# Attention loop: two steps' value products in one TensorE block, maxima over two PSUM banks, output multiply on GpSimd, three q/k buffers

## The chip, the cores and the metric

One NeuronCore of one Trainium2 chip runs the whole kernel. The metric is the device time of an execution in microseconds (us). TensorE is written PE, VectorE DVE, ScalarE ACT, GpSimd POOL and SyncE SP, as the profile does.

## The reference

The program is one graph-attention layer, a transformer layer with modulated layer norms, and an MLP, on x of 2 x 2048 x 512. The change touches only the self-attention of the second layer, 16 heads of 32 columns over 2048 positions:

```python
q, k, v = jnp.moveaxis(qkv, 2, 0)
scale = HD ** (-0.5)
attn = jnp.einsum('blhd,bmhd->bhlm', q, k) * scale
attn = jax.nn.softmax(attn, axis=-1)
out = jnp.einsum('bhlm,bmhd->blhd', attn, v).reshape(B, L, D)
```

## The kernel before

The kernel is a chain of phases (set-up, graph attention, q/k/v projection, attention, output projection, MLP); each ends in a barrier. Only the attention phase is changed.

**Groups, halves, steps.** A group is one pair of heads of one batch entry: `NG` = 16 groups. A group has `ST` = 32 steps in two halves of `MT` = 16. A half covers 1024 of the query positions (for two heads, so four column blocks of 512), a step covers 128 key positions. In each step four units c = 0 to 3 do this:

- a score matmul (`pS`, 128 keys x 512 queries, line 1261), which waits for the exponential that last read its PSUM bank; there are three banks `pS`
- ACT's exponential of it into `prob` (line 1104); `prob` has `PR` = 4 buffers
- a maxima matmul (`pM`, line 1213) of a later group, and its row maximum on DVE over 512 columns (line 1147). The maxima are needed before a group's scores start: they are put into two extra rows of `qs`, so that the score matmul subtracts them. There are three banks `pM`.

**The values block.** Between c = 2 and c = 3 PE does the step before: `behind` issues four narrow matmuls (`pO` += V x prob, 32 output rows each, line 1228), and in the five steps of a half that are in `SUMMED` four more with a column block of ones (`pZ`, line 1234), which add up the softmax denominators. The probabilities of the other eleven steps (`ADDED`) are added up by POOL (line 1083, 128x2048), and `finish` puts that sum through the ones once per half, in a block of its own.

**End of a half.** ACT copies `pO` to `oc` and `pZ` to `rec`, DVE inverts `rec` in four pieces (line 1169, one per step) and multiplies (line 1177, `output`), and ACT's queue stores.

**Group change.** Six steps before a group ends, all maxima of the next group are done: DVE takes `top` (line 1151), PE transposes it into one `pM` bank (line 1219), DVE splits it into two parts (`parts`, lines 1158, 1160), and SP stores them into `qs`.

PE issues everything in the order of the code; its waits are semaphores with constants or loop registers. Group 0's maxima have no scores to go with: they are a stretch of maxima matmuls alone ahead of the loop. The last group has no maxima to go with: its steps are scores and values alone.

Of the kernel before, what the change touches and what calls it, by code (L numbers as in the profile page):

```python
# [8 lines left out]
ALU = mybir.AluOpType  # L9
# [916 lines left out]
def attention_phase(nc, io, keep):  # L926

    with ExitStack() as ctx:
# [5 lines left out]
        NM = 2 * MT * 4  # L937
        MS = NM // ST
        LEAD = 6
        EARLY = MS  # L940
        U = 4
        PR = 4

        ADDED = [0, 1, 2, 4, 5, 6, 8, 9, 11, 12, 13]
        NA = len(ADDED) - 1
        FINISH = 2
        INVERT = 4
        STORE = 10
        SUMMED = [t for t in range(MT) if t not in ADDED]
# [9 lines left out]
        mx = m.sb("mx", [P, 32, 4])  # L959
# [4 lines left out]
        zero = m.sb("zero", [P, 1])  # L964
        pS = [m.ps(f"pS{i}") for i in range(3)]
        pM = [m.ps(f"pM{i}") for i in range(3)]
# [4 lines left out]
        top_ready, nm_hi, step_done, added, o_done, o_copied = [  # L971
            m.sem(x) for x in ("top_ready", "nm_hi", "step_done", "added", "o_done", "o_copied")]
# [9 lines left out]
        def m_unit(g, step, c):  # L982


            ahead = 1 if step < ST - LEAD else 2
            return (g + ahead, (step + LEAD) % ST * MS + c) if before(g, NG - ahead) else None

        def turn(g):


            return g * (NM + 1) + NM + (EARLY if before(g, NG - 1) else 0)

        def tile(g, n):

            return g * (NM + 1) + n - (1 if n < EARLY and at_least(g, 1) else 0)

        def bank(g, n):
            return pM[(n - (1 if n < EARLY and at_least(g, 1) else 0)) % 3]

        def turned(g):  # L1000

            return pM[(NM + (EARLY if before(g, NG - 1) else 0)) % 3]
        assert (NM + 1) % 3 == 0

        def groups(eng, body):


            for g in range(U):
                body(g, g, lambda j: (g + j) // 2)
            with eng.Fori(1, NG // U - 1) as i:  # L1010
                for k in range(U):
                    body(i * U + k, k, lambda j: i * (U // 2) + (k + j) // 2)
            for g in range(NG - U, NG):
                body(g, g % U, lambda j: (g + j) // 2)

        def half_before(g, step):

            return 2 * g + step // MT - 1

        @block.sync  # L1020
        def _(sp):
            def load(k, hp):
                at = slice(k % 2 * S, (k % 2 + 1) * S)
                for i, part in enumerate((0, 0, 1)):
                    sp.dma_start(raw(qs[k][i * HD:(i + 1) * HD]), q_v[part, bass.ds(hp, 1), :, :, at]
                                 .rearrange("a p h n -> (a p) h n")).then_inc(loaded[k], 16)
                for i, part in enumerate((0, 1, 0)):
                    sp.dma_start(raw(ks[k][i * HD:(i + 1) * HD]), k_v[part, bass.ds(hp, 1), :, :, at]
                                 .rearrange("a p h n -> (a p) h n")).then_inc(loaded[k], 16)

            def load_v(k, hp):
                sp.dma_start(V[k][:], v_v[:, k, :, bass.ds(hp * 2 * HD, 2 * HD)]).then_inc(v_loaded[k], 16)

            def rows(g, k):

                sp.wait_ge(m_read, turn(g) + 1)
                for h in range(2):
                    sp.dma_start(raw(qs[k][KD + h:KD + h + 1]).rearrange("a h (t n) -> a (h t) n", n=P),
                                 raw(nm[:, h, :])).then_inc(top_rows[k], 16)

            load(0, 0)
            load(1, 0)
            load_v(0, 0)
            load_v(1, 0)
            load(2, 1)
            load(3, 1)
            rows(0, 0)

            def body(g, k, pair):
                if at_least(g, 1):  # L1050
                    sp.wait_ge(step_done, g * ST)
                    if before(g, NG - U + 1):
                        load((k - 1) % U, pair(U - 1))
                    if before(g, NG - 1):
                        load_v((k + 1) % 2, pair(1))
                if before(g, NG - 1):
                    rows(g + 1, (k + 1) % U)
            groups(sp, body)

        @block.gpsimd  # L1060
        def _(pool):
            nc.gpsimd.memset(ones[:], 1.0).then_inc(cleared, 1)  # L1062
            nc.gpsimd.memset(zero[:], 0.0).then_inc(cleared, 1)
            for k in range(U):
                pool.wait_ge(cleared, 2 + k)
                nc.gpsimd.memset(raw(ks[k][KD:KD + 2]), 1.0).then_inc(cleared, 1)
            pool.wait_ge(cleared, 2 + U)

            def body(g, k, pair):
                for half in range(2):  # L1070
                    for i in range(1, NA + 1):
                        step = half * MT + ADDED[i]
                        n = (g * 2 + half) * NA
                        pool.wait_ge(exp_done, (g * ST + step) * 4 + 4)
                        new = prob[step % PR]
                        if i == 1:
                            if at_least(g, 1):
                                pool.wait_ge(z_done, g * 2 + half - 1)
                            old = prob[(half * MT + ADDED[0]) % PR]
                        else:  # L1080
                            pool.wait_ge(added, n + i - 1)
                            old = acc[half]
                        nc.gpsimd.tensor_tensor(acc[half][:], old[:], new[:], ALU.add).then_inc(added, 1)  # L1083
            groups(pool, body)

        @block.scalar
        def _(act):
            def free(g, step):

                if step < PR and not at_least(g, 1):  # L1090
                    return
                act.wait_ge(step_done, g * ST + step - PR + 1)
                half, t = divmod((step - PR) % ST, MT)
                if t in ADDED:
                    whole = (g if step >= PR else g - 1) * 2 + half
                    act.wait_ge(added, whole * NA + max(1, ADDED.index(t)))

            def body(g, k, pair):
                for step in range(ST):
                    free(g, step)  # L1100
                    for c in range(4):
                        n = 4 * step + c
                        act.wait_ge(s_done, g * 4 * ST + n + 1)
                        nc.scalar.activation(prob[step % PR][:, c, :], pS[n % 3][:], ACT.Exp, scale=SCALE).then_inc(exp_done, 1)  # L1104
                        if step % MT == 0 and c == 2 and (step or at_least(g, 1)):
                            copy(half_before(g, step))
                    if step % MT == FINISH + 1 and (step >= MT or at_least(g, 1)):
                        copy_sums(half_before(g, step))
                    if step == STORE and at_least(g, 1):
                        store(2 * g - 1, (k - 1) % U, pair(-1), 1)  # L1110
                    if step == MT + STORE:
                        store(2 * g, k, pair(0), 0)

            def copy(n):

                act.wait_ge(o_done, n + 1)
                if at_least(n, 1):
                    act.wait_ge(o_ready, n)
                nc.scalar.activation(oc[:], pO[:], ACT.Identity).then_inc(o_copied, 1)

            def store(n, k, hp, half):

# [648 lines left out]
```

## Time and profile before

| | us |
|---|---|
| median of 3 runs | 3696.48 (3693.08 to 3698.31) |
| profiled execution, span from first to last instruction | 3696.8 |
| attention phase, first maxima matmul to last store | 897.8 to 2798 |
| PE busy over the span | 3452.4 (93%) |
| DVE, ACT, POOL busy | 2266.1, 1552.4, 1775.8 |

The profiled execution has no time listed of its own; its span lies within the range of the three runs, so the span is used for it. In the timelines a row gives the start of the first instruction of a run of like instructions, the time from there to the end of the last, the engine, line, operation, tiles and shapes, how many, and in brackets how long the engine was idle before it and who released it. A matmul's duration is modelled; differences of starts are what to read. Busy time of PE thus doesn't tell how full it is.

### The profile page before, as it was taken

The page shows a single profiled execution, that of the slowest core. Times are in us where ns is not written, and L with a number is a line of the kernel's source. Part 1 is how long each engine was busy: PE and PEld are TensorE (multiplying, and loading weights), DVE is VectorE, ACT ScalarE, POOL GpSimd, SP SyncE. Part 2 cuts the span into 40 slices and gives each one's busy share as a digit, 9 for nine tenths or more (in the row PEclk, how much of TensorE's full clock was granted, in tenths as well). Part 3 has the DMA queues.
Part 4 walks back from the last instruction along what each step waited for, and adds up shares of the span by engine and source line. Part 5 has one row for each costly group of instructions (what it writes and reads, how often), then busy time and mean ns, then how long its engine had stood idle before and what let it go on. Part 6 is the DMA issues. An engine that isn't in the chain of part 4 may idle for free. (4 is left out here: it accounts for less than half of the span.)

```text
span 3696.8 us, 51173 instructions
## 1 busy us (share of the span) xinstructions
PE 3452.4 (93%) x17516; PEld 2197.3 (59%) x17516; DVE 2266.1 (61%) x3547; ACT 1552.4 (42%) x2751; POOL 1775.8 (48%) x527
## 2 busy tenths in 40 slices
PE   7899996997999999999999999999995779999999
PEld 6488885775544444444444444444434658888887
DVE  1378874444978788788788887887715932222222
ACT  0111114341166666666656666666662242222222
POOL 1033321001288788787887887877885500000000
PEclk9999998997699999999999999999997889999999
DMA  4122224446201222102222022200004641111100
GB/s 163 66 93 88 91 80 172 172 158 183 46 17 34 43 47 44 38 16 44 47 48 44 7 44 47 47 10 13 7 6 154 216 146 68 40 40 40 37 32 23
DMA packets 158137, 250.59 MB, mean 68 GB/s; under 512 B 46939, under 2 KB 68699, under 8 KB 151774
## 3 DMA queue, kind: packets, MB, share of 16 engines
q1 hardware_dynamic: 147166, 230.96, 21.1%
q10 hardware_dynamic: 10752, 16.79, 1.5%
q8 instruction: 128, 2.10, 0.2%
q14 instruction: 91, 0.75, 0.1%
HBM read 158.89 MB, written 88.08 MB: 67 GB/s over the span
## 5 line engine op out<-in xcount | busy, mean ns | idle before, releaser
L1147 DVE TENSOR_REDUCE att_mx<-att_pM 128x1 f32<-128x512 f32 x2048 | 1267.9, 680 | 336.2 <-PE att_pM L1213 334.0
L1104 ACT ACTIVATE att_prob<-att_pS 128x512 f32<-128x512 f32 x2048 | 1080.4, 601 | 772.8 <-PE att_pS L1261 765.2
L1083 POOL TENSOR_TENSOR att_acc<-att_acc,att_prob 128x2048 f32<-128x2048 f32 x288 | 1327.5, 4609 | 129.2 <-ACT att_prob L1104 104.1
L1213 PE MATMUL att_pM<-att_ks,att_qs 96*128 96x512 f32 x2048 | 855.1, 432 | 54.7 <-DVE att_mx L1147 33.6
L1261 PE MATMUL att_pS<-att_qs,att_ks 98*128 98x512 f32 x2048 | 868.8, 430 | 10.2 <-ACT att_prob L1104 8.0
L1261 PEld LDWEIGHTS att_pS<-att_qs,att_ks 98*128 98x128 f32 x2048 | 386.2, 190 | 555.1 <-ACT att_prob L1104 385.7
L1228 PE MATMUL att_pO<-att_prob,att_V 128*32 128x512 f32 x4096 | 548.7, 608 | 0.7 <-ACT att_prob L1104 0.7
L1213 PEld LDWEIGHTS att_pM<-att_ks,att_qs 96*128 96x128 f32 x2048 | 405.4, 198 | 200.5 <-DVE att_mx L1147 120.3
L1627 DVE TENSOR_TENSOR mlp_us<-mlp_tu,mlp_us 128x512 fp32r<-128x512 f32 x128 | 89.7, 700 | 536.0 <-ACT mlp_us L1600 536.0
L1670 PE MATMUL mlp_pu<-mlp_hs,mlp_W 128*128 128x512 f32 x1536 | 370.7, 391 | 18.9 <-DVE mlp_W L1619 18.9
L1689 PE MATMUL mlp_pa<-mlp_W,mlp_us 128*128 128x512 f32 x1536 | 368.8, 389 | 0.0
L1670 PEld LDWEIGHTS mlp_pu<-mlp_hs,mlp_W 128*128 128x128 f32 x1536 | 289.7, 189 | 79.4 <-issue 19.2
L1612 POOL TENSOR_TENSOR mlp_hs<-mlp_hf,mlp_hs 128x512 fp32r<-128x512 f32 x32 | 41.1, 1287 | 598.6 <-ACT mlp_hs L1578 598.6
L1689 PEld LDWEIGHTS mlp_pa<-mlp_W,mlp_us 128*128 128x128 f32 x1536 | 288.5, 188 | 59.7
L1599 ACT ACTIVATE mlp_tu<-mlp_pu,keep_cols 128x512 f32<-128x512 f32 x128 | 88.2, 689 | 503.4 <-PE mlp_pu L1670 503.4
L1083 POOL TENSOR_TENSOR att_acc<-att_prob 128x2048 f32<-128x2048 f32 x32 | 146.6, 4580 | 291.5 <-ACT att_prob L1104 291.5
L921 PE MATMUL qkv_pq<-qkv_hs,qkv_W 128*128 128x512 f32 x768 | 187.3, 400 | 2.4 <-DVE qkv_hs L861 2.4
L1169 DVE RECIPROCAL att_rec<-att_rec 128x128 f32<-128x128 f32 x128 | 119.6, 940 | 105.3 <-ACT att_rec L1133 105.3
L1228 PEld LDWEIGHTS att_pO<-att_prob,att_V 128*32 128x32 f32 x4096 | 81.0, 108 | 166.6 <-issue 93.2
L1234 PE MATMUL att_pZ<-att_prob,att_ones 128*32 128x512 f32 x1280 | 166.6, 592 | 0.0
L921 PEld LDWEIGHTS qkv_pq<-qkv_hs,qkv_W 128*128 128x128 f32 x768 | 144.9, 192 | 32.4 <-issue 2.8
L1062 POOL MEMSET att_ones<- 128x32 f32 x1 | 0.1, 124 | 304.8 <-POOLq L107 304.8
(181 smaller groups left out, 2984.7 us busy)
## 6 DMA issues: line engine op xcount, KB each, us to landing
qk_d<-qkv_qs SPq DMA_DIRECT2D x64, 512.0 KB, 2.7
att_qs<-qk_d SPq DMA_DIRECT2D x48, 512.0 KB, 7.4
att_ks<-qk_d SPq DMA_DIRECT2D x48, 512.0 KB, 13.8
gat_xT<-in_xT SPq DMA_DIRECT2D x32, 256.0 KB, 3.1
gat_xrow<-in_x SPq DMA_DIRECT2D x32, 256.0 KB, 2.8
x_d<-gat_x SPq DMA_DIRECT2D x32, 256.0 KB, 2.1
qkv_xr<-x_d SPq DMA_DIRECT2D x8, 1024.0 KB, 5.8
v_d<-qkv_vs SPq DMA_DIRECT2D x32, 256.0 KB, 2.0
```

The costliest lines, as they stand in the source:

```text
L921: last = nc.tensor.matmul(out[:], a, r, start=n + c == 0, stop=n == 2 and c == DC - 1)
L1083: nc.gpsimd.tensor_tensor(acc[half][:], old[:], new[:], ALU.add).then_inc(added, 1)
L1104: nc.scalar.activation(prob[step % PR][:, c, :], pS[n % 3][:], ACT.Exp, scale=SCALE).then_inc(exp_done, 1)
L1147: nc.vector.tensor_reduce(mx[:, n // 4, n % 4:n % 4 + 1], bank(g, n)[:], AX.X, ALU.max).then_inc(m_read, 1)
L1169: nc.vector.reciprocal(rec[:, at], rec[:, at]).then_inc(inverted, 1)
L1213: nc.tensor.matmul(bank(g, n)[:], qs[k][0:KD, h, t * P:(t + 1) * P], ks[k][0:KD, h, mc * 512:(mc + 1) * 512], start=True, stop=True).then_ ...
L1228: last = nc.tensor.matmul(pO[c * HD:(c + 1) * HD, :], V[k % 2][:, mt, (c // 2) * HD:(c // 2 + 1) * HD], prob[step % PR][:, c, :], start=mt ...
L1234: last = nc.tensor.matmul(pZ[c * HD:(c + 1) * HD, :], ones[:], src[:, c, :], start=first, stop=last_one, skip_group_check=True)
L1261: nc.tensor.matmul(pS[n % 3][:], ks[k][:, h, mt * P:(mt + 1) * P], qs[k][:, h, lc * 512:(lc + 1) * 512], start=True, stop=True).then_inc(s ...
L1627: nc.vector.tensor_tensor(us[j % 2][:, 1, :], tu[j % 2][:], us[j % 2][:, 0, :], ALU.subtract).then_inc(u_lo, 1)
L1670: last = nc.tensor.matmul(pu[j % 4][:], W1[:, k, c, j * P:(j + 1) * P], hs[s][:, w, c, :], start=q + c == 0, stop=q == 2 and c == DC - 1)
L1689: last = nc.tensor.matmul(pa[nt][:], us[j % 2][:, k, nt * P:(nt + 1) * P], W2[:, w, j, :], start=j + q == 0, stop=j == MC - 1 and q == 2)
```

## The change

- `behind` now takes a pair of steps: one block of 8 narrow matmuls (or 12, 16) at each even step, between c = 2 and c = 3, where there were two blocks. `finish` goes into the block of step 4. `prob` has 8 buffers instead of 4 for that.
- The maxima matmuls write two banks (`pM` is [128, 2, 512], two of them, four banks in all), and DVE takes one maximum over 1024 columns. `pM` took three banks before. The scores have two banks `pS`, where they had three: eight banks in all as before.
- The output multiply is POOL's (`scale`), after its sixth addition of the next half. The stores are on SP's queue, not ACT's. ACT's copies sit behind c = 1 of steps 1 and 5.
- `qs` and `ks` have three buffers, not four; a load is issued two groups ahead, not three.
- The loop over groups is written out (no hardware loop).
- `SUMMED` is [7, 9, 11, 14, 15], where it was [3, 7, 10, 14, 15].

```diff
-        U = 4
-        PR = 4
-
-        ADDED = [0, 1, 2, 4, 5, 6, 8, 9, 11, 12, 13]
+        U = 3
+        PR = 8
+
+        SUMMED = [7, 9, 11, 14, 15]
+        ADDED = [t for t in range(MT) if t not in SUMMED]
-        pS = [m.ps(f"pS{i}") for i in range(3)]
-        pM = [m.ps(f"pM{i}") for i in range(3)]
+        pS = [m.ps(f"pS{i}") for i in range(2)]
+        pM = [m.ps(f"pM{i}", [P, 2, 512]) for i in range(2)]
+        def wait_bank(pe, at):
+            if at >= 2:
+                pe.wait_ge(m_read, at - 1)
+            def scale(n):
+
+                g, half = divmod(n, 2)
+                pool.wait_ge(o_copied, n + 1)
+                pool.wait_ge(inverted, (n + 1) * 4)
+                if g >= 1:
+                    pool.wait_ge(o_stored[half], g * 64)
+                nc.gpsimd.tensor_tensor(o[half][:], oc[:], rec[:], ALU.mult).then_inc(o_ready, 1)
+                        if step % MT == 1 and c == 1 and n >= 0:
+                            copy(n)
+                        if step % MT == 2 * FINISH + 1 and c == 1 and n >= 0:
+                            copy_sums(n)
-                nc.vector.tensor_reduce(mx[:, n // 4, n % 4:n % 4 + 1], bank(g, n)[:], AX.X, ALU.max).then_inc(m_read, 1)
+                nc.vector.tensor_reduce(mx[:, q // 2, q % 2:q % 2 + 1], bank(at)[:], AX.XY, ALU.max).then_inc(m_read, 1)
+            def behind(g, p):
+
+                for step in (2 * p, 2 * p + 1):
+                    last = values(g, step)
+                    t, n = step % MT, 2 * g + step // MT
                     if t == MT - 1:
                         last.then_inc(o_done, 1)
+                    if t in SUMMED:
+                        if t == SUMMED[0] and n:
+                            pe.wait_ge(z_read, n)
+                        last = sums(prob[step % PR], t == SUMMED[0], False)
+                last.then_inc(pair_done, 1)
+            def scores(g, step, c):
+
+                at = (g * ST + step) * 4 + c
+                half, mt = divmod(step, MT)
+                k, h, lc = g % U, c // 2, 2 * half + c % 2
+                if at >= 2:
+                    pe.wait_ge(exp_done, at - 1)
+                nc.tensor.matmul(pS[at % 2][:], ks[k][:, h, mt * P:(mt + 1) * P], qs[k][:, h, lc * 512:(lc + 1) * 512],
+                                 start=True, stop=True).then_inc(s_done, 1)
+                pair = m_pair(g, step, c // 2)
+                if pair:
+                    maxima(*pair, c % 2)
+                    for c in range(4):
+                        scores(g, step, c)
+                        if step % 2 == 0 and c == 2 and (g or step):
+                            before = g * ST // 2 + step // 2 - 1
+                            behind(before // (ST // 2), before % (ST // 2))
+                            if step % MT == 2 * FINISH and (g or step >= MT):
+                                finish(2 * g + step // MT - 1)
```

On PE, early in the first group before the change: a values block (`pO`), four score matmuls (`pS`) each with a maxima matmul (`pM`), and the next block.

```order
L1228 MATMUL att_pO<-att_prob,att_V 32x512 x4
L1261 MATMUL att_pS<-att_qs,att_ks 128x512
L1213 MATMUL att_pM<-att_ks,att_qs 128x512
L1261 MATMUL att_pS<-att_qs,att_ks 128x512
L1213 MATMUL att_pM<-att_ks,att_qs 128x512
L1261 MATMUL att_pS<-att_qs,att_ks 128x512
L1213 MATMUL att_pM<-att_ks,att_qs 128x512
L1261 MATMUL att_pS<-att_qs,att_ks 128x512
L1213 MATMUL att_pM<-att_ks,att_qs 128x512
L1228 MATMUL att_pO<-att_prob,att_V 32x512 x4
```

The same engine and place after the change, from the end of one block's run of pairs into the next block; the run has eight pairs of score and maxima matmul between blocks, of which the last two stand ahead of the block here and the first two behind it.

```order
L1262 MATMUL att_pS<-att_qs,att_ks 128x512
L1210 MATMUL att_pM<-att_ks,att_qs 128x512
L1262 MATMUL att_pS<-att_qs,att_ks 128x512
L1210 MATMUL att_pM<-att_ks,att_qs 128x512
L1227 MATMUL att_pO<-att_prob,att_V 32x512 x8
L1262 MATMUL att_pS<-att_qs,att_ks 128x512
L1210 MATMUL att_pM<-att_ks,att_qs 128x512
L1262 MATMUL att_pS<-att_qs,att_ks 128x512
L1210 MATMUL att_pM<-att_ks,att_qs 128x512
```

Two blocks of four became one of eight, and the pairs between blocks went from four to eight.

On DVE, before, the reciprocals at the end of a half with the row maxima (`att_mx`) between them, then the output multiply (`att_o`), `top` and the two parts:

```order
L1169 RECIPROCAL att_rec<-att_rec 128x128
L1147 TENSOR_REDUCE att_mx<-att_pM 128x1 x4
L1169 RECIPROCAL att_rec<-att_rec 128x128
L1147 TENSOR_REDUCE att_mx<-att_pM 128x1 x4
L1177 TENSOR_TENSOR att_o<-att_oc,att_rec 128x512
L1147 TENSOR_REDUCE att_mx<-att_pM 128x1 x5
L1151 TENSOR_REDUCE att_top<-att_mx 128x32
L1147 TENSOR_REDUCE att_mx<-att_pM 128x1 x4
L1158 CAST att_nm<-att_pM 32x128
L1160 TENSOR_TENSOR att_nm<-att_pM,att_nm 32x128
```

And after the change:

```order
L1174 RECIPROCAL att_rec<-att_rec 128x128
L1153 TENSOR_REDUCE att_mx<-att_pM 128x1 x2
L1174 RECIPROCAL att_rec<-att_rec 128x128
L1157 TENSOR_REDUCE att_top<-att_mx 128x32
L1153 TENSOR_REDUCE att_mx<-att_pM 128x1 x2
L1165 CAST att_nm<-att_pM 32x128
L1167 TENSOR_TENSOR att_nm<-att_pM,att_nm 32x128
```

The multiply is gone from DVE, four maxima of 512 columns are two of 1024, and the reciprocals run up to the step of `top`.

## Rows read from the trace of the kernel before

**Rows 1.** The page: busy time of each engine.

```profile
PE 3452.4 (93%) x17516; PEld 2197.3 (59%) x17516; DVE 2266.1 (61%) x3547; ACT 1552.4 (42%) x2751; POOL 1775.8 (48%) x527
```

**Rows 2.** Waits: who waited for whom, total us, times, longest us.

```profile
PEld att_pS L1261 <- ACT att_prob L1104: 385.7, 483, 2.1
PEld att_pM L1213 <- DVE att_mx L1147: 120.3, 277, 1.8
```

**Rows 3.** Timeline of one plain step of the loop, weight loads left out.

```profile
1501.06 0.51 PE L1261 MATMUL att_pS<-att_qs,att_ks 98*128 98x512 f32 x1
1501.40 0.40 PE L1213 MATMUL att_pM<-att_ks,att_qs 96*128 96x512 f32 x1
...
1501.60 2.07 ACT L1104 ACTIVATE att_prob<-att_pS 128x512 f32<-128x512 f32 x4 [1.02 <-PE att_pS L1261]
...
1501.84 2.48 DVE L1147 TENSOR_REDUCE att_mx<-att_pM 128x1 f32<-128x512 f32 x4 [0.59 <-PE att_pM L1213]
...
1502.81 0.39 PE L1213 MATMUL att_pM<-att_ks,att_qs 96*128 96x512 f32 x1
...
1503.13 1.06 PE L1228 MATMUL att_pO<-att_prob,att_V 128*32 128x512 f32 x8
1504.13 0.50 PE L1261 MATMUL att_pS<-att_qs,att_ks 98*128 98x512 f32 x1
```

**Rows 4.** Timeline of the finishing sums in a block of their own.

```profile
1504.79 1.06 PE L1234 MATMUL att_pZ<-att_acc,att_ones 128*32 128x512 f32 x8
1505.78 0.50 PE L1261 MATMUL att_pS<-att_qs,att_ks 98*128 98x512 f32 x1
```

**Rows 5.** Timeline of a values block with sums behind the values.

```profile
1537.46 1.06 PE L1228 MATMUL att_pO<-att_prob,att_V 128*32 128x512 f32 x8
...
1539.31 0.50 PE L1261 MATMUL att_pS<-att_qs,att_ks 98*128 98x512 f32 x1
```

**Rows 6.** Timeline of one step of the last group, without maxima.

```profile
2702.87 0.96 PE L1261 MATMUL att_pS<-att_qs,att_ks 98*128 98x512 f32 x3
2703.41 2.06 ACT L1104 ACTIVATE att_prob<-att_pS 128x512 f32<-128x512 f32 x4 [0.54 <-PE att_pS L1261]
...
2704.06 0.50 PE L1261 MATMUL att_pS<-att_qs,att_ks 98*128 98x512 f32 x1 [0.23 <-ACT att_prob L1104]
...
2705.49 0.97 PE L1261 MATMUL att_pS<-att_qs,att_ks 98*128 98x512 f32 x3
```

**Rows 7.** Timeline of the stretch of maxima alone.

```profile
929.72 6.66 DVE L1147 TENSOR_REDUCE att_mx<-att_pM 128x1 f32<-128x512 f32 x11
...
930.46 0.28 PEld L1213 LDWEIGHTS att_pM<-att_ks,att_qs 96*128 96x128 f32 x1 [0.31 <-DVE att_mx L1147]
```

**Rows 8.** By tile: duration ns min/median/max, first and last start.

```profile
L1151 DVE TENSOR_REDUCE att_top<-att_mx x16: 286/286/289, 975.3 to 2668.6; 128x32 f32<-128x128 f32 x16
...
L1083 POOL TENSOR_TENSOR att_acc<-att_acc,att_prob x288: 4500/4582/4906, 1001.5 to 2785.4; 128x2048 f32<-128x2048 f32 x144
...
L1169 DVE RECIPROCAL att_rec<-att_rec x128: 894/943/953, 1059.3 to 2795.0; 128x128 f32<-128x128 f32 x128
...
L1177 DVE TENSOR_TENSOR att_o<-att_oc,att_rec x32: 692/3036/4677, 1072.8 to 2796.1; 128x512 f32<-128x512 f32 x32
```

**Rows 9.** By tile, 1200 to 2600 us: the copy of pO.

```profile
L1119 ACT ACTIVATE att_oc<-att_pO x25: 597/597/597, 1214.9 to 2577.9; 128x512 f32<-128x512 f32 x25
```

**Rows 10.** Timeline of the attention's end: the last finishing sums.

```profile
2789.92 1.93 PE L1234 MATMUL att_pZ<-att_acc,att_ones 128*32 128x512 f32 x8 [3.89 <-POOL att_acc L1083]
```

**Rows 11.** By tile: landing of DMAs into qs.

```profile
DMA to landing us min/median/max: 2.1/4.8/21.1
```

**Rows 12.** Windows: busy us of engines, PE clock, DMA share, GB/s.

```profile
880.00:990.00 110.00, 91.83 (x155) 44.49 (x156) 91.28 (x155) 1.28 (x1) 14.18 (x6) 0.50 0.59 124
...
2695.00:2775.00 80.00, 73.86 (x387) 24.79 (x387) 16.07 (x10) 55.67 (x107) 74.45 (x17) 0.98 0.03 7
```

More of the change, by code:

```diff
@@ L980, in attention_phase, with m_pair @@
         o_v = io["o_d"].rearrange("(g h p) (b n) -> g h p b n", h=2, p=HD, b=B)
[L982 removed]
+        def m_pair(g, step, half):
             ahead = 1 if step < ST - LEAD else 2
[L986 to L995 removed]
@@ L997, in bank @@
[L997 to L1014, printed above, removed]
@@ L1016, in half_before, with fill @@
-        def half_before(g, step):
-            return 2 * g + step // MT - 1
+            return (g + ahead, (step + LEAD) % ST * 2 + half) if g + ahead < NG else None
+        place = {}
+        def fill(what):
+            place[what] = len(place)
+        for q in range(NQ):
+            fill((0, q))
+        for q in range(EARLY):
+            fill((1, q))
+        fill("turned 0")
+        for q in range(EARLY, LEAD * 2):
+            fill((1, q))
+        for g in range(NG):
+            for step in range(ST):
+                if step == ST - LEAD + 1 and g + 1 < NG:
+                    fill(f"turned {g + 1}")
+                for half in range(2):
+                    if m_pair(g, step, half):
+                        fill(m_pair(g, step, half))
@@ L1043, in _ @@
[L1043 to L1057, printed above, removed]
@@ new lines, in _ @@
+            load(0)
+            load(1)
+            load_v(0)
+            load_v(1)
+            load(2)
+            rows(0)
+            for g in range(NG):
+                if g >= 1:
+                    sp.wait_ge(pair_done, g * ST // 2)
+                    if g + 2 < NG:
+                        load(g + 2)
+                    if g + 1 < NG:
+                        load_v(g + 1)
+                    store(2 * g - 1)
+                if g + 1 < NG:
+                    rows(g + 1)
+                store(2 * g)
@@ L1060, in _ @@
+            store(2 * NG - 1)
+            for x in o_stored:
+                sp.wait_ge(x, 16 * 4 * NG)
         @block.gpsimd
@@ L1099, in body @@
+            for g in range(NG):
                 for step in range(ST):
+                    n = 2 * g + step // MT - 1
                     free(g, step)
                     for c in range(4):
[L1102 to L1119, printed above, removed]
@@ L1182, in _ @@
-            for n in range(EARLY):
-                maxima(1, n)
-            parts(0, 0)
-            for n in range(EARLY, LEAD * MS):
-                maxima(1, n)
-            def body(g, k, pair):
+            for q in range(NQ):
+                maxima(0, q)
+            top_of(0)
+            for q in range(EARLY):
+                maxima(1, q)
+            parts(0)
+            for q in range(EARLY, LEAD * 2):
+                maxima(1, q)
+            for g in range(NG):
                 for step in range(ST):
-                    if step == ST - LEAD and before(g, NG - 1):
+                    n = 2 * g + step // MT - 1
+                    if step == ST - LEAD and g + 1 < NG:
@@ L1200, in _ @@
-            groups(dve, body)
-            for c in range(5):
-                invert(2 * NG - 1, 1, NG - 1, c)
+                    if step == ST - LEAD + 1 and g + 1 < NG:
+                        parts(g + 1)
+                    for half in range(2):
+                        if m_pair(g, step, half):
+                            maxima(*m_pair(g, step, half))
+                    if 0 <= step % MT - INVERT < 4 and n >= 0:
+                        invert(n, step % MT - INVERT)
+            for c in range(4):
+                invert(2 * NG - 1, c)
@@ L1296, in proj_phase @@
+            behind(NG - 1, ST // 2 - 1)
+            finish(2 * NG - 1)
 def proj_phase(nc, io, keep):
```

251 lines of the change are left out of this document (110 added, 141 removed).

## The prediction

> **What bounds the kernel now.** I read the page first: PE is busy 93% of the span, DVE 61%, POOL 48%, ACT 42% [rows 1]. Busy shares don't settle it, since a matmul's end is modelled, so I went to the waits and then to the timeline of the attention loop. The waits list PE's weight loads for scores behind ACT and for maxima behind DVE [rows 2], but the first of these is mostly wrongly named: in a plain step [rows 3] those gaps stand behind the values block, where the array is at work. What the reader is to see in that step is the differences of PE's starts. From the block to the next score 1503.13 to 1504.13, 1.00 us; score to maxima matmul 0.34; then six more matmuls at (1502.81 - 1501.40) / 6 = 0.235; from the last to the next block 0.32. Sum 1.00 + 0.34 + 1.41 + 0.32 = 3.07 us, with no wait in it: PE's own issue sets the plain step. ACT (four exponentials in 2.07) and DVE (four maxima in 2.48) are idle 1.02 and 0.59 before their first [rows 3].
>
> A block of eight narrow matmuls takes 1.85 until the next score [rows 5], so four more narrow ones cost 0.85, and a block 0.15 on top. With 0.34 and 0.32 in place of 0.235 at its two ends, a block costs 0.15 + 0.105 + 0.085 = 0.34 besides its work.
>
> A half lasts (2577.9 - 1214.9) / 24 = 56.8 us [rows 9]. From the parts: 16 x 3.07 = 49.1, five times sums 4.3, the finishing block 0.99 + 0.32 less 0.13 for what it shares = 1.2 [rows 4], together 54.6. The rest, 2.2, is DVE's fault for the most part (four reciprocals of 0.94 and the multiply, whose median is 3.04 and whose least is 0.69 [rows 8], all in front of maxima that PE's banks wait for), and some clock.
>
> **The multiply and a rule.** 0.69 at the end, when POOL is idle, against 3.04 amid POOL's additions: the two engines block one another there [rows 8]. The Trainium skill, SBUF — State Buffer, "Who interferes with whom", says that a DVE instruction with two SBUF inputs contends with a GpSimd instruction that reads SBUF; by that rule the multiply leaves DVE for good reason, and the trace agrees. On POOL it costs about 4.58 / 4 = 1.15 [rows 8]; POOL then has 10 x 4.58 + 1.15 = 47 us of work in a half of over 56, and eight buffers of prob to be late with. Nothing waits for it. That takes most of the multiply's share out of the 2.2, which I put at 1.4.
>
> **The merged block.** Eight blocks a half go: 8 x 0.34 = 2.7 saved, and the finishing one's 0.34. That is the whole of what merging can give, if nothing else waits.
>
> **The banks.** Something else does. A score bank isn't free when the score is done but when ACT has read it. The last group shows the time round a bank [rows 6]: score at 2702.87, its exponential at 2703.41 (0.54), and the fourth score, which needs that bank, at 2704.06: 1.19 from start to start, with PE idle for it (0.23) and 0.10 of weight load bare (0.50 instead of 0.40). Three banks let four scores through, as one is done each time ahead of the block and three behind. With two banks and eight scores in a run, PE can issue two scores in 1.19, where its own pace with maxima between is 4 x 0.235 = 0.94.
>
> Likewise for the maxima. A maximum of 512 columns follows the last after (6.66 - 2.48) / 7 = 0.60 [rows 3, 7], and the weight load that it releases comes 0.74 after its start (930.46 - 929.72) [rows 7]. The wide one isn't in the trace. Its slope from 128 to 512 columns is (0.69 - 0.286) / 384 = 1.05 ns a column [rows 3, 8], so 512 more cost 0.54: 1.14 for the wide one, 1.19 if the second bank costs as much as an instruction, which is the upper bound. I take 1.14. The bank pair is released 1.28 after its start.
>
> Now the double step, with time 0 at the first score's load behind the block (matmul itself at 0.10; exponential 0.44 after a matmul, at least 0.49 after the last; score load possible 0.65 after an exponential's start; maximum 0.44 after the second maxima matmul). Scores: 0.10, 0.57, then behind the bank 0.54 + 0.65 + 0.10 = 1.29, 1.78, 2.48, 2.97, 3.67, 4.16: three times 1.19 and once 0.49. DVE starts at 0.77, 1.96, 3.15, 4.34; so the maxima matmuls behind a bank pair come at 2.05 + 0.10 = 2.15, 3.34 and 4.53, the last one 0.13 later than PE would. Then 0.32 to the block: 4.85, and 1.85 for it: 6.70. Before: 6.14. So each double step becomes **0.56 longer**, not 0.34 shorter. Without DVE's share it is 6.57; with 1.19 for the wide maximum 6.77. If the bare weight loads overlap better than I take it, 6.46. The merged block doesn't hide this, as both queues run dry in it and fill up only in the run behind it.
>
> **Other terms per half.** Copies of pO and pZ now sit within the run (c = 1), 0.60 each [rows 9], in a chain of ACT that has 0.2 of slack a round: +0.5 each, 1.0 (0 to 1.2). Four reciprocals of 0.94 [rows 8], two in each of two double steps, where DVE has 4 x 1.14 = 4.6 of 6.7 to do: the next maxima are up to 0.94 late each, and I take 1.5 (0 to 3.8). Group change: the transposed tile takes one of two bank pairs, and the next maxima matmul has to wait until the one before is read, 0.44 + 1.28 + 0.10 = 1.8 after it instead of 0.8: +1.0 a group, 0.5 a half (0 to 1). Clock as now, 0.3.
>
> New half: 8 x 6.70 = 53.6, sums 4.25, finishing sums in a block 0.85, 1.0, 1.5, 0.5, 0.3: **62.0 against 56.8**, +5.2.
>
> **No cost.** Loads: issued at a group's start and needed 25 steps, over 75 us, later; the slowest lands after 21.1 [rows 11]. Stores and rows on SP: each store waits for a multiply that is done well before the group change. The written-out loop does the same work.
>
> **Sum.** 28 halves x 5.2 = 146. First half, without copies and finish, 8 x 0.56 = 4.5. Last groups: the double step without maxima is 4.48 + 1.85 = 6.33 against 2 x (2705.49 - 2702.87) = 5.24 [rows 6], +1.09; 2 halves x 8 of these 17.5, and the half before, where maxima end, 6. Maxima alone: 76 wide of 1.14 to 1.18 for 152 of 0.60, -3. End: PE's 3.9 for POOL [rows 10] goes, since POOL catches up, and a longer last block comes: -2. Together +169 on the span of 3696.8, which stands 0.3 above the median of the runs: **3865 us**.
>
> **Rivals.**
> - Faster (chance 0.08). The turnaround of 1.19 is no limit, because the exponential can follow closer when scores come regularly; it decides at 0.94 a round. Then a double step is 6.14 - 0.34 = 5.80, a half 56.8 - 2.7 - 0.34 - 1.4 = 52.4, so 32 x 4.4 = 141 less: 3556. For it: merged blocks do save their ends. Against it: 1.19 is seen with ACT idle ahead of it [rows 6], so nothing is left to follow closer.
> - No change (0.03): double step near 6.14, if only every other round waits; 3690 to 3704.
> - The same mechanism, with a DVE that is the limit (within the forecast, 0.25): the wide maximum at 1.19 and reciprocals at their full 3.8: +0.07 x 8 + 2.3 = 2.9 a half, 3950 at most; half of that 3910.
> - Clock (0.05). PE now idles for a moment in every round. In the maxima-only stretch, where it idles in each, the granted clock was 0.50; in the last group, where it idles once a step, 0.98 [rows 12]. Were the loop at half clock for a tenth of its time, the work of some 85% of 62 us would double there: 32 x 62 x 0.85 x 0.1 = +169, 4034. The new loop is like the last group, not like the stretch of maxima: its PE has as much work in a period (16 x 0.235 + 1.7 of 6.7). The Trainium skill, TensorE: Matmul & The Clock Gate, "A second HAM failure mode: psum-queue depth-cycling", says that cycling through PSUM banks can let PE micro-idle often enough that the clock oscillates; no row here shows it at this load.
>
> **How the numbers follow.** The forecast, slower by the bank rounds, has 0.84. Its own unknowns: double step 6.46 to 6.77 gives -61 to +18, reciprocals -45 to +70, copies and group change -45 to +20. They don't all fall one way: 3790 to 3915. The rivals outside it hold 0.16, within the two tenths. What a measurement of this kernel can tell from no change is about 0.2%, 7 us. Faster 0.08, same 0.03, slower 0.89 (forecast and clock).
>
> **What would show it.** Right: in the timeline scores at 0.49 and 0.70 by turns between blocks, with PE's loads released by ACT at each second one; eight narrow matmuls and the next score 1.85 apart; halves of about 62; a wide maximum of 1.22 (0.69 + 0.54) at distances of 1.14 or more; the multiply on POOL near 1.15. Wrong, if scores keep 0.47 in a run, if the wide maximum takes over 1.3, or if the clock row shows long stretches at half.

## Result and the profile after

The changed kernel takes 3888.86 us (median of 4 runs, 3886.79 to 3890.1), against 3697.39 for the kernel before: ratio 1.0519 with a 95% interval of 1.0501 to 1.0536. It is slower by 191 us; the forecast was 3865 us (+169), range 3790 to 3915.

The page and the waits of the changed kernel, to set beside [rows 1, 2] (columns of the waits: total us, times, longest us):

```profile
PE 3598.6 (93%) x17516; PEld 2181.8 (56%) x17516; DVE 2127.6 (55%) x2491; ACT 1636.5 (42%) x2751; POOL 1800.1 (46%) x557
```

```profile
PEld att_pS L1262 <- ACT att_prob L1138: 366.0, 1031, 1.0
...
PEld att_pM L1210 <- DVE att_mx L1153: 141.3, 241, 1.3
```

PE's share is 93% as before, with 17516 instructions as before, in 191 us more: in these traces a matmul whose weight load had to wait is shown as 0.50 us instead of 0.40, so busy time hides part of the loss. The count tells more: 1031 score loads are put down to ACT where 483 were, and those of before were mostly gaps behind a block.

The timeline of the run of eight pairs between two blocks, in the changed kernel, with the weight loads left out; it answers to [rows 3]:

```profile
1547.88 0.50 PE L1262 MATMUL att_pS<-att_qs,att_ks 98*128 98x512 f32 x1
...
1548.42 4.77 ACT L1138 ACTIVATE att_prob<-att_pS 128x512 f32<-128x512 f32 x8 [1.92 <-PE att_pS L1262]
1548.45 0.40 PE L1262 MATMUL att_pS<-att_qs,att_ks 98*128 98x512 f32 x1
1548.65 4.77 DVE L1153 TENSOR_REDUCE att_mx<-att_pM 128x1 f32<-128x1024 f32 x4 [1.93 <-PE att_pM L1210]
...
1549.07 0.50 PE L1262 MATMUL att_pS<-att_qs,att_ks 98*128 98x512 f32 x1
...
1549.63 0.47 PE L1262 MATMUL att_pS<-att_qs,att_ks 98*128 98x512 f32 x1
...
1550.27 0.47 PE L1262 MATMUL att_pS<-att_qs,att_ks 98*128 98x512 f32 x1
...
1552.73 1.07 PE L1227 MATMUL att_pO<-att_prob,att_V 128*32 128x512 f32 x8
```

Scores stand at 1547.88, 1548.45, 1549.07, 1549.63, 1550.27: two in 1.19 to 1.20, as worked out. The view joins ACT's eight exponentials into one row of 4.77, and DVE's four wide maxima into another ((4.77 - 1.22) / 3 = 1.18 apart). Neither engine is at its own limit there: eight exponentials take 4.13 with three score banks (first experiment), and wide maxima follow one another after 1.14 in the stretch of maxima alone. Both engines go at the pace of the rounds, and PE waits for each of them in turn. The run takes 4.85 until the block, as forecast. A plain double step (from the starts of the scores, the median) is 6.73 us; forecast 6.70, before 6.14.

By tile, the wide maximum, the multiply on POOL and the copy of pO (this last one between 1200 and 2600 us, as in [rows 9]):

```profile
L1153 DVE TENSOR_REDUCE att_mx<-att_pM x1024: 1159/1224/1229, 904.7 to 2822.7; 128x1 f32<-128x1024 f32 x171
```

```profile
L1078 POOL TENSOR_TENSOR att_o<-att_oc,att_rec x32: 1260/1278/1284, 1099.0 to 2985.9; 128x512 f32<-128x512 f32 x32
```

```profile
L1122 ACT ACTIVATE att_oc<-att_pO x22: 590/591/593, 1250.5 to 2544.5; 128x512 f32<-128x512 f32 x22
```

A half is (2544.5 - 1250.5) / 21 = 61.6 us; forecast 62.0, before 56.8. The 28 full halves give 137 of the 191 us.

**Where the rest is.** The last group and the maxima alone. A window over the last group, before [rows 12] and now (us, then busy us of PE, PEld, DVE, ACT, POOL, the granted clock, DMA share, GB/s):

```profile
2845.00:2970.00 125.00, 109.97 (x454) 33.77 (x454) 6.78 (x8) 67.85 (x122) 85.78 (x22) 0.84 0.02 5
```

Its halves take 67.7 and 64.5 where they took 47.8 and 50.3 before, and where the forecast's +17.5 for both comes to 57.8 each. The granted clock is 0.84 instead of 0.98. It goes back and forth between its two levels there, 1.2 GHz (0.50) and 2.4 GHz (1.00), as two stretches show:

```profile
2872.00:2878.00 6.00, 5.74 (x20) 1.62 (x21) 2.69 (x4) 1.93 (x4) 5.86 (x2) 0.50 0.01 3
2886.00:2898.00 12.00, 10.22 (x47) 3.32 (x39) 0.00 (x0) 7.86 (x14) 7.41 (x2) 1.00 0.08 21
```

The stretch of maxima alone, with two wide bank pairs, as a timeline to set beside [rows 7]:

```profile
916.14 0.50 PEld L1210 LDWEIGHTS att_pM<-att_ks,att_qs 96*128 96x128 f32 x2 [0.91 <-DVE att_mx L1153]
...
917.40 2.36 DVE L1153 TENSOR_REDUCE att_mx<-att_pM 128x1 f32<-128x1024 f32 x2 [0.18 <-PE att_pM L1210]
...
918.68 0.50 PEld L1210 LDWEIGHTS att_pM<-att_ks,att_qs 96*128 96x128 f32 x2 [0.91 <-DVE att_mx L1153]
```

From load to load 2.54 for two wide maxima, so 1.27 for 1024 columns against 2 x 0.60 = 1.20 before: the stretch is 5.7 us longer, not 3 shorter. The changes per place: full halves +137, first half +3.5, the half before the last group +7.7, last group +34.1, maxima alone +5.7, the attention's end -3.4, the phases ahead +5.7 and behind +1.1; together 191. The 5.7 ahead need not be the change's: attention began at 902 to 905 us in most profiles below, also of kernels that are close to the one before, and at 898 in two (the kernel before and the one with the multiply alone on GpSimd). A comparison of two single profiles carries these 6 us with it.

### The profile page after: what moved, and what is told of

It is laid out like the page before. It is cut to its first block and busy times, and to the rows that moved or that the text cites. A ratio compares the mean times of both kernels' runs of the same rounds, so it can differ in the third digit from the quotient of the medians.

```text
span 3888.3 us, 45175 instructions
## 1 busy us (share of the span) xinstructions
PE 3598.6 (93%) x17516; PEld 2181.8 (56%) x17516; DVE 2127.6 (55%) x2491; ACT 1636.5 (42%) x2751; POOL 1800.1 (46%) x557
## 5 line engine op out<-in xcount | busy, mean ns | idle before, releaser
L1153 DVE TENSOR_REDUCE att_mx<-att_pM 128x1 f32<-128x1024 f32 x1024 | 1220.6, 1217 | 620.7 <-PE att_pM L1210 620.2
L1138 ACT ACTIVATE att_prob<-att_pS 128x512 f32<-128x512 f32 x2048 | 1171.0, 598 | 895.9 <-PE att_pS L1262 855.6
L1262 PE MATMUL att_pS<-att_qs,att_ks 98*128 98x512 f32 x2048 | 961.9, 472 | 35.3 <-ACT att_prob L1138 31.9
L1210 PE MATMUL att_pM<-att_ks,att_qs 96*128 96x512 f32 x2048 | 887.2, 442 | 76.7 <-DVE att_mx L1153 55.7
L1210 PEld LDWEIGHTS att_pM<-att_ks,att_qs 96*128 96x128 f32 x2048 | 397.6, 199 | 236.6 <-DVE att_mx L1153 141.3
L1227 PE MATMUL att_pO<-att_prob,att_V 128*32 128x512 f32 x4096 | 513.1, 614 | 0.0
L1690 PEld LDWEIGHTS mlp_pa<-mlp_W,mlp_us 128*128 128x128 f32 x1536 | 288.3, 188 | 59.9
L1227 PEld LDWEIGHTS att_pO<-att_prob,att_V 128*32 128x32 f32 x4096 | 108.6, 111 | 231.4 <-issue 124.2
## 6 DMA issues: line engine op xcount, KB each, us to landing
att_ks<-qk_d SPq DMA_DIRECT2D x48, 512.0 KB, 13.3
```

Of the source, the lines that this page charges most:

```text
L1138: nc.scalar.activation(prob[step % PR][:, c, :], pS[at % 2][:], ACT.Exp, scale=SCALE).then_inc(exp_done, 1)
L1153: nc.vector.tensor_reduce(mx[:, q // 2, q % 2:q % 2 + 1], bank(at)[:], AX.XY, ALU.max).then_inc(m_read, 1)
L1210: last = nc.tensor.matmul(bank(at)[:, i, :], qs[k][0:KD, h, t * P:(t + 1) * P], ks[k][0:KD, h, mc * 512:(mc + 1) * 512], start=True, stop= ...
L1227: last = nc.tensor.matmul(pO[c * HD:(c + 1) * HD, :], V[g % 2][:, mt, (c // 2) * HD:(c // 2 + 1) * HD], prob[step % PR][:, c, :], start=mt ...
L1262: nc.tensor.matmul(pS[at % 2][:], ks[k][:, h, mt * P:(mt + 1) * P], qs[k][:, h, lc * 512:(lc + 1) * 512], start=True, stop=True).then_inc( ...
L1690: last = nc.tensor.matmul(pa[nt][:], us[j % 2][:, k, nt * P:(nt + 1) * P], W2[:, w, j, :], start=j + q == 0, stop=j == MC - 1 and q == 2)
```

## Experiments

Ratios are to the kernel before, in runs on the same chip; times of a half are worked out from the copies of pO between 1200 and 2600 us, and those of double steps and of the last group's halves from the scores' starts (medians for the double steps).

**Banks of before in the changed kernel.** Three score banks, three narrow maxima banks; merged blocks and the rest stay.

```diff
-        pS = [m.ps(f"pS{i}") for i in range(2)]
-        pM = [m.ps(f"pM{i}", [P, 2, 512]) for i in range(2)]
+        pS = [m.ps(f"pS{i}") for i in range(3)]
+        pM = [m.ps(f"pM{i}") for i in range(3)]
-                nc.vector.tensor_reduce(mx[:, q // 2, q % 2:q % 2 + 1], bank(at)[:], AX.XY, ALU.max).then_inc(m_read, 1)
+                for i in range(2):
+                    at = place[g, q] + i
+                    col = q % 2 * 2 + i
+                    dve.wait_ge(m_done, at + 1)
+                    nc.vector.tensor_reduce(mx[:, q // 2, col:col + 1], bank(at)[:], AX.X, ALU.max).then_inc(m_read, 1)
```

> The changed kernel with the banks of before: three score banks, three narrow maxima banks with a maximum of 512 columns each; merged blocks, multiply on GpSimd, three q/k buffers and the written-out loop stay. Bank theory (the turnaround of two score banks and of two wide bank pairs costs the time): the loop comes back to about 56.2 to 56.7 us a half, the kernel to 3690 to 3705. Rival, side-effect theory (the late copies, stores on SP's queue, three buffers or the unrolled loop cost the time): it stays near 3890. Naive merge theory (blocks save 0.34 each once the banks are right): 3600.

3705.9 us, ratio 1.0018 (1.0007 to 1.0029), a half 56.6. The banks account for the loss; late copies, stores on SP, three q/k buffers and the written-out loop don't. Nor does merging give the time that the naive line expected. The timeline of its run shows why:

```profile
1456.24 4.13 ACT L1141 ACTIVATE att_prob<-att_pS 128x512 f32<-128x512 f32 x8 [1.64 <-PE att_pS L1265]
...
1456.48 4.87 DVE L1158 TENSOR_REDUCE att_mx<-att_pM 128x1 f32<-128x512 f32 x8 [1.32 <-PE att_pM L1214]
...
1459.61 0.50 PE L1214 MATMUL att_pM<-att_ks,att_qs 96*128 96x512 f32 x1
1460.04 1.92 PE L1230 MATMUL att_pO<-att_prob,att_V 128*32 128x512 f32 x16
```

DVE does eight maxima in 4.87, 0.60 apart, while PE could issue eight pairs in 3.8. With four pairs in a run, three free banks cover the difference; with eight they don't, and PE waits (maxima matmul at 0.50). The waits of this run (us, times, longest) name DVE where the changed kernel's name ACT:

```profile
PEld att_pM L1214 <- DVE att_mx L1158: 312.6, 973, 1.0
...
PEld att_pS L1265 <- ACT att_prob L1141: 67.5, 211, 0.8
```

The double step is 6.19 instead of 6.14: what the block ends save, DVE's pace takes back. The two double steps in which DVE has two reciprocals of 0.94 besides its eight maxima are 0.8 longer each. So the ratio near 1 is a sum of gains and losses. The last experiment below has the multiply on GpSimd, the merged finishing sums, the stores on SP and the written-out loop without merging, and takes 3651.57. Against it merging, with the eight prob buffers, three q/k buffers and late copies that came with it, costs 54 us even with the banks of before (a half 56.6 against 54.8).

**Two score banks, narrow maxima in four banks.**

> The changed kernel with two score banks, but narrow maxima in four single banks. It splits the bank theory: if the score banks set the time, a plain double step is 6.57 and a half about 60.4, the kernel 3845 to 3860, most of the loss kept. If the wide maxima set it, the loss goes: about 3700.

3823.63, ratio 1.0332 (1.0314 to 1.0351), below the 3845 to 3860 expected; a half is 59.8, 0.6 less than expected. The double step is 6.73, the same as with wide maxima and 0.16 above the 6.57 expected: the score banks alone set it. Its waits:

```profile
PEld att_pS L1265 <- ACT att_prob L1141: 533.9, 1518, 1.0
...
PEld att_pM L1214 <- DVE att_mx L1158: 45.3, 146, 0.4
```

The changed kernel's other 1.9 us a half, which the wide maxima cost, lies in the steps with reciprocals and at the group change, which here cost next to nothing. With the longer stretch of maxima alone, the wide maxima cost 65 us. Going from three score banks and three for maxima to two and four cost 118 (3705.9 to 3823.63).

**Two score banks in the kernel before.** The only edit:

```diff
-        pS = [m.ps(f"pS{i}") for i in range(3)]
+        pS = [m.ps(f"pS{i}") for i in range(2)]
-                    if n >= 3 or at_least(g, 1):
-                        pe.wait_ge(exp_done, g * 4 * ST + (n - 2 if n >= 3 else (-1, 0, -2)[n]))
-                    nc.tensor.matmul(pS[n % 3][:], ks[k][:, h, mt * P:(mt + 1) * P], qs[k][:, h, lc * 512:(lc + 1) * 512],
+                    if n >= 2 or at_least(g, 1):
+                        pe.wait_ge(exp_done, g * 4 * ST + n - 1)
+                    nc.tensor.matmul(pS[n % 2][:], ks[k][:, h, mt * P:(mt + 1) * P], qs[k][:, h, lc * 512:(lc + 1) * 512],
```

> The kernel before with two score banks in place of three and nothing else changed. Score-bank theory: a step of four pairs gets two rounds of 1.19 in place of free issue, about 60.6 a half, +136 us, 3833. Rival (the loss needs the merged block's long run of eight pairs): within 20 us of before.

3865.27, ratio 1.0443 (1.0423 to 1.0464), +164. The third score bank is worth that much in the short run of four too; the rival falls. It is 32 us more than expected: the median half is 61.3, not 60.6 (the mean is 61.9, in a profile of its slowest run, 10 us above the median). The step in which ACT's queue issues the stores went from 4.10 to 5.80 us, where a score waits 1.14 for ACT; and the last group's halves take 58.5 and 60.2. Part of the gap between mean and median is the clock, which fell to 0.50 for a moment four times in the full loop, for instance here:

```profile
1979.00:1985.00 6.00, 5.54 (x21) 1.66 (x20) 1.98 (x3) 2.28 (x4) 0.00 (x0) 0.50 0.01 3
```

The turnaround is seen plainly:

```profile
1497.66 0.50 PE L1261 MATMUL att_pS<-att_qs,att_ks 98*128 98x512 f32 x1
...
1498.20 1.79 ACT L1104 ACTIVATE att_prob<-att_pS 128x512 f32<-128x512 f32 x3 [1.07 <-PE att_pS L1261]
...
1498.86 0.50 PE L1261 MATMUL att_pS<-att_qs,att_ks 98*128 98x512 f32 x1
```

Score at 1497.66, its exponential 0.54 later, the score that reuses the bank at 1498.86: 1.20.

**One block per step in the changed kernel.** The copy of pO moves with it, to c = 2 of step 0.

```diff
-                        if step % MT == 1 and c == 1 and n >= 0:
+                        if step % MT == 0 and c == 2 and n >= 0:
                             copy(n)
-                        if step % 2 == 0 and c == 2 and (g or step):
-                            before = g * ST // 2 + step // 2 - 1
-                            behind(before // (ST // 2), before % (ST // 2))
+                        if c == 2 and (g or step):
+                            before = g * ST + step - 1
+                            behind(before // ST, before % ST)
```

> The changed kernel with one values block per step again (a block behind c = 2 of each step), the copy of pO behind c = 2 of step 0; banks and all else as changed. Theory that each block lets both queues run empty and so gives two scores for free: the unmerged kernel is faster than the changed one, by about 1.4 us a half, 3845, although it pays 0.34 for eight more blocks. Rival (the block's own ends are what counts): slower by 8 x 0.34 x 32 = 87, 3975.

3857.71, ratio 1.042 (1.04 to 1.044): 31 us faster than the changed kernel, and 13 us slower than expected. A half is 61.3 against 61.6, where 1.4 less was expected. Two plain steps take 2 x 3.48 = 6.96 where the double step takes 6.73; merging saves 0.23 there, so the expectation was wrong on the plain step. In return the steps with copies and reciprocals are no longer than plain ones any more. 23 of the 31 us come from the last group, whose halves are 54.9 and 54.4, with the clock full:

```profile
2838.00:2940.00 102.00, 88.33 (x448) 27.57 (x447) 6.78 (x8) 67.15 (x124) 86.61 (x21) 1.00 0.02 6
```

**The third score bank with wide maxima.** Eight banks don't hold three score banks, four for wide maxima, pO and pZ. So both runs leave out the sums on TensorE and pZ, and take the denominators from part of the added probabilities, so their output isn't the layer's; the second uses the free bank for scores.

```diff
-                    if t in SUMMED:
-                        if t == SUMMED[0] and n:
-                            pe.wait_ge(z_read, n)
-                        last = sums(prob[step % PR], t == SUMMED[0], False)
-                nc.scalar.activation(rec[:], pZ[:], ACT.Identity).then_inc(z_read, 1)
+                nc.scalar.activation(rec[:], acc[n % 2][:, 0, :], ACT.Identity).then_inc(z_read, 1)
```

> The changed kernel without the softmax denominators on TensorE (no narrow matmuls of ones, no pZ; the denominators are taken from part of the added probabilities instead, so the output isn't the reference's). It frees one PSUM bank; this run leaves it unused, as the base of the next one. PE loses 5 x 0.85 + 0.85 = 5.1 a half, all of which shows, since the block lies apart from the runs that wait: about 56.5 a half, 3725. A plain double step stays at 6.7.

> As the run without denominators, with the freed bank as a third score bank: wide maxima and merged blocks stay. Score-bank theory: the turnaround no longer limits, the wide maxima do (two bank pairs in 2.3 to 2.4): a double step near 6.35 to 6.5, a half near 54.5, 65 to 80 us under the run with two score banks. If the wide bank pairs are the limit anyway: within 15 us of it.

3736.28 (3725 was expected) and 3659.29, ratios 1.01 (1.0083 to 1.0116) and 0.9898 (0.9882 to 0.9915): 77 us apart, within the 65 to 80, but spread otherwise than thought. A half goes from 56.5 to 55.1, not to 54.5, and a double step from 6.72 only to 6.63, not to 6.35 to 6.5. So the two bank pairs of wide maxima limit it nearly as much as the two score banks did. The timeline of the run with three score banks shows PE held by DVE:

```profile
1453.61 0.51 PE L1210 MATMUL att_pM<-att_ks,att_qs 96*128 96x512 f32 x1 [0.16 <-DVE att_mx L1153]
...
1456.34 1.93 PE L1227 MATMUL att_pO<-att_prob,att_V 128*32 128x512 f32 x16
1458.19 0.50 PE L1245 MATMUL att_pS<-att_qs,att_ks 98*128 98x512 f32 x1
```

A good 33 of the 77 us are the last group, where scores alone run and the third bank frees them (halves of 47.6 and 48.5 against 65.1 and 64.1). Part of these 33 is the clock again: over the last group it is 0.77 with two score banks and 0.92 with three.

**A matmul that nobody reads behind each score of the last group.**

```diff
+                elif g == NG - 1:
+                    nc.tensor.matmul(pM[0][:, 0, :], qs[k][0:KD, h, mt * P:(mt + 1) * P], ks[k][0:KD, h, 0:512],
+                                     start=True, stop=True)
```

> The changed kernel with a matmul that nobody reads behind each score of the last group, where there are no maxima (2048 score matmuls as before, 128 more wide ones in all). Clock theory (the last group's 67.7 and 64.5 us a half instead of 57 come from granted clock at half, as PE has too little to do there): the clock stays full, halves near 58.5, the kernel about 15 us faster, 3874. Rival (waiting on banks in a new order makes those halves long): no gain, or some us slower.

3875.69 (3874 was expected), ratio 1.0479 (1.0461 to 1.0496), 13 us faster than the changed kernel although it does 128 more matmuls. The halves are 59.9 and 59.0, and the window over the last group:

```profile
2845.00:2960.00 115.00, 113.54 (x582) 47.42 (x583) 6.78 (x8) 72.52 (x129) 90.02 (x22) 1.00 0.02 5
```

The clock is 1.00. The two halves are 13.3 us shorter together, out of the 16.6 by which they stood above the forecast; the rest is open, and the added matmuls are in it. So most of the excess is the clock, and giving PE more to do in the last group brings the clock back. What of the pattern lets it fall isn't told apart: the last group's clock is 0.84 with two score banks and merged blocks, 0.93 with three banks and merged blocks, and 1.00 with two banks and a block per step.

**What the change had right, on the kernel before.** The multiply alone on GpSimd, with the stores on ACT's queue moved from step 10 to step 12; then also the finishing sums in the block of step 3; then also the stores on SP's queue with the loop written out.

```diff
-        STORE = 10
+        STORE = 12
-                nc.vector.tensor_tensor(o[half][:], oc[:], rec[:], ALU.mult).then_inc(o_ready, 1)
+                nc.gpsimd.tensor_tensor(o[half][:], oc[:], rec[:], ALU.mult).then_inc(o_ready, 1)
```

```diff
+                    if step % MT == FINISH + 1 and (step >= MT or at_least(g, 1)):
+                        finish(g, step)
                     scores(step, 3)
-                    if step % MT == FINISH and (step >= MT or at_least(g, 1)):
-                        finish(g, step)
```

> The kernel before with the output multiply alone moved to GpSimd (after its fifth addition of the next half; stores stay on ACT's queue, at step 12). The forecast's term for it: 1.4 us a half saved, 45 us, 3652. Rival (DVE's other work fills the gap and the multiply was hidden): within 8 us of before.

> The same with the finishing sums placed right behind the values block of step 3 instead of a block of their own. A block's ends cost 0.34: another 0.33 x 32 = 10.7 us saved, 3641. Rival (the sums wait for GpSimd's last addition there, or the copy behind them comes late): nothing saved or slower.

3666.08, ratio 0.9914 (0.9893 to 0.9935), and 3661.75, ratio 0.9893 (0.9873 to 0.9913). The multiply is worth 35 us by the medians, less than the 45 expected; the six runs of that kernel lie in two sets, three at 3658 to 3660 and three at 3672 to 3676. In the trace the step that DVE's multiply had lengthened (step 9) went from 4.46 to 3.06, the 1.4 of the forecast, but 0.35 came back in steps 13 and 14. There ACT's queue issued the four stores between the last exponential of step 12 and the first of step 13, which are the first and second behind a values block. The run with the merged finish shows it too:

```profile
1478.57 0.60 ACT L1116 ACTIVATE att_prob<-att_pS 128x512 f32<-128x512 f32 x1 [1.00 <-PE att_pS L1263]
...
1478.74 1.79 ACTq L1138 DMA_DIRECT2D o_d<-att_o  x4
...
1480.80 3.04 ACT L1116 ACTIVATE att_prob<-att_pS 128x512 f32<-128x512 f32 x6 [1.63 <-PE att_pS L1263]
```

That pause of ACT isn't new. In the kernel before, the stores held ACT as long, two steps earlier, and cost nothing:

```profile
1364.53 1.76 ACTq L1126 DMA_DIRECT2D o_d<-att_o  x4
...
1366.39 1.57 ACT L1104 ACTIVATE att_prob<-att_pS 128x512 f32<-128x512 f32 x3 [1.27 <-PE att_pS L1261]
1366.95 1.04 PE L1234 MATMUL att_pZ<-att_prob,att_ones 128*32 128x512 f32 x8
1367.92 0.50 PE L1261 MATMUL att_pS<-att_qs,att_ks 98*128 98x512 f32 x1
```

The block that follows there has sums behind the values (1366.95), so it is 0.85 longer, and the next score (1367.92) comes no later than it would without the stores; the block in step 13 has no sums. The cost of 0.35 came with the move of the stores. In step 11, with two score banks, the same pause cost 1.7.

The merged finish is worth 4 us by the medians, within the intervals of each other. The two traces show more: 9.6 us less over the 28 full halves, near the 10.7 expected, but attention begins 6 us later in the second.

> The kernel before with the multiply on GpSimd and the merged finishing sums (as in the run before), and the four output stores of a half issued from SP's queue instead of ACT's, with the loop over groups written out. In the run before, the four stores held ACT for 1.79 us between a first and a second exponential, and the step behind was 0.29 and 0.06 longer. Theory: 0.35 a half goes, 11 us, 3650. Rival (the code written out costs or gains something by itself, or SP's stores come late): more than 8 us away from that.

3651.57 (3650 was expected), ratio 0.9864 (0.9842 to 0.9886): 1.4% faster than the kernel before and 6% faster than the changed one. A half is (2584.4 - 1215.3) / 25 = 54.8, by this row (copy of pO, 1200 to 2600 us):

```profile
L1134 ACT ACTIVATE att_oc<-att_pO x26: 597/597/598, 1215.3 to 2584.4; 128x512 f32<-128x512 f32 x26
```

The forecast's parts give 54.6 - 0.3 = 54.3 for a half in which PE never waits; 0.5 is left. The two steps that the stores had lengthened are plain again (3.07 each), which gives the 0.35. The stores and the written-out loop weren't tried apart. In the kernel before, four of the full halves are 1.3 to 1.9 us longer than their neighbours, three of them with a moment of lower clock (0.57 from 1529 to 1533 us); here none is. Whether the written-out loop makes that difference isn't shown.

## Why the prediction was right

- **The score banks.** Right in mechanism: the turnaround is 1.19 to 1.20. Shown by the kernel before with two score banks (+164 us) and by the changed kernel with the old banks (no loss).
- **The double step.** 6.73 against 6.70 is partly luck, since two errors cancel. The forecast put the second score 0.47 behind the first, though its own reading of a plain step gives 0.34 + 0.235 = 0.575 behind a bare load, and the trace has 0.57. That moves the fourth, sixth and eighth score by 0.1 and brings the 6.57 for the score banks alone to 6.67. The 0.13 that it added for DVE isn't there.
- **The wide maxima.** 1.14 apart where they follow one another (2.36 - 1.22 in the stretch of maxima alone), as taken; the duration is 1.224, forecast 1.22. But "without DVE's share it is 6.57" failed: with narrow maxima in four banks the double step was 6.73 all the same, and with three score banks and wide maxima 6.63. The two limits overlap, they don't add up.
- **Merging.** The forecast gave merging 8 x 0.34 = 2.7 a half, if nothing else waits, and blamed the banks for the rest. With two score banks it saved 0.23 a plain double step, but the kernel with one block per step was still 31 us faster as a whole. With three banks each it cost 1.8 a half (54.8 to 56.6), since a run of eight pairs is longer than DVE can follow. So of the 191 us some 54 would have come with the old banks too, hidden by what the multiply, the merged finish and the stores gave back.
- **Odd jobs.** Copies cost 0.8 a half (forecast 1.0) and reciprocals 1.35 (1.5), from steps with them against plain ones; the group change 0.55 a half (0.5). The changed kernel's group change, to set beside the bare step, with the reduction that PE waits for:

```profile
1595.19 0.27 PE L1218 MATMUL att_pM<-keep_ident,att_top 128*32 128x128 f32 x1
...
1596.67 0.50 PE L1210 MATMUL att_pM<-att_ks,att_qs 96*128 96x512 f32 x1 [0.98 <-DVE att_mx L1153]
```

- **The multiply.** 1.4 a half was forecast. On the kernel before its step became 1.4 shorter, and 35 us / 32 = 1.1 is left, with the 0.35 of the moved stores in it. On POOL it takes 1.28, forecast 1.15.
- **Mis-sized terms.** The last group was put at +17.5 and gave +34.1; filling PE brought back 13. The clock rival had been worked out for a tenth of the loop; it came true in the last group alone, which the forecast had held up as the safe case. Maxima alone were put at -3 and gave +5.7: the term took DVE's pace and left out that two pairs are a round trip of their own, 1.26 from load to maximum at half clock and 1.28 back. The full halves were put at +146 and gave +137, so part of the good total is that errors of both signs met.
- The rivals "faster" (3556) and "no change" fall: no run with two score banks kept 0.94 a round. Halves of 61.6 are on the side of the forecast, not of its variant with DVE as the limit (3910 to 3950).

Not tried: more than two bank pairs for wide maxima, as the banks don't suffice.

## What to carry to other kernels

Count the banks by the time round a bank (matmul to reader to next matmul, here 1.19 us) against the producer's pace between two pauses (here 0.94 for two scores), and for the longest run without a pause: merging two pauses into one saves their ends but doubles the run, and what the reader could catch up in the pause comes back as a wait. Try each part of a bundle alone; here the multiply off DVE, the merged finishing sums and the stores off ACT's queue were worth 1.4% together and were buried under what the banks and the merging cost. Four stores issued from ACT's queue held ACT for 1.8 us, and whether that shows depends on where they fall and on the banks: nothing in a step with a long block, 0.35 us in a plain step, 1.7 with two score banks.

## What the runs showed of the hardware

- In the last group the granted clock was 0.84 with two score banks and merged blocks, 1.00 with one block per step and the same banks, and 1.00 with merged blocks and a filler matmul behind each score. In the filled case PE's loads waited for ACT as often as before (87 times against 80 from 2857 to 2970 us), but for less time (29.5 us against 40.8). The Trainium skill, TensorE: Matmul & The Clock Gate, "A second HAM failure mode: psum-queue depth-cycling", describes a clock that oscillates because PE is idle for moments while it cycles through PSUM banks. The trace agrees for scores alone, where the clock went between 0.50 and 1.00. It doesn't for the full loop of the changed kernel, whose clock stayed at its upper level (2.4 GHz, 1.00) from 1010 to 2825 us although 1031 of PE's score loads are put down to ACT.
- The multiply of two SBUF operands took 3.04 us on DVE amid POOL's additions [rows 8] and 1.28 on POOL, and the additions took as long as before (median 4.58 both times).
